# Stage six attention: the context scores as one product per head inside the row-tiled group, instead of one block-diagonal product

## The chip, the cores and the metric

The kernel runs on one core of a Trainium2 chip. It is written by hand, engine by engine: TensorE (PE), VectorE (DVE), ScalarE (ACT), GpSimd (POOL) and SyncE (SP) each have their own instruction list, and semaphores order them against one another. The metric is the device time of one execution in microseconds (us), the median of several executions.

## The reference, cut to what matters

The program is four layers, each of a gated cross attention and a gated feed-forward part, on x of shape 2 x 1024 x 256. They are computed as eight stages, 0 to 7. The change touches stage six, the cross attention of the last layer:

```
q = layer_norm(latents) @ Wq            # latents = layer-normed x, 2 x 1024 rows
kv = concat(layer_norm(ctx), layer_norm(latents)) @ Wkv
sim = einsum('bhid,bhjd->bhij', q * scale, k)     # 16 heads of 64
attn = softmax(where(mask, sim, max_neg))
out = einsum('bhij,bhjd->bhid', attn, v) @ Wout
```

So every one of the 1024 query rows of a batch element attends to 1101 columns: 1024 tokens (self) and 77 rows of context, and only the context columns can be masked. All is float32.

## The kernel before

Stage six walks over 128 units (`NU`). Unit u is one tile of 128 queries (`qt = u % 8`) of one pair of heads (`n = u // 8`; 8 pairs for each of the 2 batch elements). The two heads of a pair lie in the partitions 0 to 63 (head zero) and 64 to 127 (head one) of the query tile `s6_q`, the key tile `s6_k` and the context keys `s6_kx`.

The scores of a unit fill PSUM banks 0 to 4: head zero's 1024 token columns in banks 0 and 1, head one's in banks 3 and 4, and both heads' 77 context columns in bank 2, head zero's at its front and head one's at its end (`s6_both` is a view of both). So each head's 1101 columns are contiguous (`s6_sc`). PE's function `scores(u)` (L1146) waits until the exponentials of the unit before have been read out of these banks (`a6_p`), then multiplies:

- the context columns of both heads in one product over all 128 partitions. For this `s6_kx` is block-diagonal, 2 x 77 columns: head zero's keys stand in partitions 0 to 63 of the first 77 columns, head one's in partitions 64 to 127 of the other 77, and the rest is zero (a POOL memset at the start of the stage, L1852);
- four products of 512 token columns, each over the 64 partitions of one head.

DVE then takes the unit up. On the first signal of `a6_s` (the context product) it adds the mask to the context columns (L2465) and reduces them to a maximum for each head (L2466). On the second signal (the last token product) it reduces each head's 1024 token columns (L2470) and takes the lower of the two negated maxima (L2471); each of these two signals `a6_mx`. ACT exponentiates each head's 1101 columns (L1728) with that as bias and signals `a6_p`.

Five further steps run in the same loop on banks 5, 6 and 7, which rotate: a step takes the bank of the step three places before it in the list and waits until that one has been copied out (`free_bank`, L1139). In iteration u, PE does `scores(u)`; two turns (transposes) of unit u-1's exponentials, `p_turn` 0 and 1, copied out by ACT (L1717); in even u, two pieces of the projections of the next head pair (`piece`, numbers j = u % 8 and j+1); in odd u, `weigh`, the product of the attention with the values; then the turn of the context columns (`ctx_turn`, L1178 and L1179), `p_turn` 2 and 3, copied out by DVE (L2492); in even u the turn of the row sums (L1186). Of the two pieces, ACT copies out the first, j, and does so between the two exponentials of unit u; DVE copies out the second (L2411, L2410), after the maxima of unit u. The pieces by j = u % 8 are: 0: queries; 2: value tiles 0 and 1 together with the context keys, and keys; 4: value tiles 2 to 5, and keys; 6: value tiles 6 to 8, and keys. For the context keys ACT has two copies, one for each block of the diagonal (L1694, L1695). Units 120 to 127 have no pieces, and a few units (60 to 67, and from 124 on) have output projections and normalisations beside the rest.

On PE a float32 product shows in the trace as two passes, each a weight load (PEld) and a MATMUL record. `link` on DVE makes the engine wait for its own instruction; an instruction without it lets the next start before it ends.

Of the kernel before, what the change touches and what calls it, by code (L numbers as in the profile page):

```python
# [12 lines left out]
ALU = mybir.AluOpType  # L13
ACT = mybir.ActivationFunctionType
AX = mybir.AxisListType

P = 128
# [34 lines left out]
def build(nc, A, out, stages=ALL_STAGES):  # L52

    ctx = ExitStack()
    with ctx:
# [3 lines left out]
        def sem(name):  # L59
            return ctx.enter_context(nc.semaphore(name))  # L60
# [28 lines left out]
        def cut(region, at, *shape, rows=P, dt=F32):  # L89

            n = int(np.prod(shape))
            words = n if dt == F32 else n // 2
            v = region[0:rows, at:at + words]
            if dt != F32:
                v = v.bitcast(dt)
            if len(shape) == 2:
                v = v.rearrange("p (a b) -> p a b", a=shape[0])
            if len(shape) == 3:
                v = v.rearrange("p (a b c) -> p a b c", a=shape[0], b=shape[1])
            return v  # L100
# [107 lines left out]
        s6_wout = cut(WE, 0, 8, D)  # L208
        s6_wq, s6_wk, s6_wv = (cut(WE, 2048 * (i + 1), KD, 8 * P) for i in range(3))
        s6_gob = cut(WE, 8192, 2, D)  # L210
        s6_kx = [cut(WE, 8704 + 154 * i, 2, C) for i in range(2)]
        s6_mk = cut(WE, 9012, B, C)
        s6_p = [[cut(WO, 1536 + 1104 * (2 * i + h), 1104) for h in range(2)] for i in range(2)]
        s6_q = [cut(WO, 5952 + 1024 * i, S) for i in range(2)]
# [86 lines left out]
        c6_mm, c6_sb = sem("c6_mm"), sem("c6_sb")  # L301
        a6_s, a6_mx, a6_p, a6_rb, o6_sd = sem("a6_s"), sem("a6_mx"), sem("a6_p"), sem("a6_rb"), sem("o6_sd")
        r6_mm, r6_act, r6_dve = sem("r6_mm"), sem("r6_act"), sem("r6_dve")
        z6_in, g6_sb, x6_b = sem("z6_in"), sem("g6_sb"), sem("x6_b")
        q5_n, q5_s, q5_w, q5_b, q5_f = sem("q5_n"), sem("q5_s"), sem("q5_w"), sem("q5_b"), sem("q5_f")
        cn6_x, cn6_tr, cn6_f = sem("cn6_x"), sem("cn6_tr"), sem("cn6_f")
        m7, gc7_mm, gc7, f7_tr, f7_add = sem("m7"), sem("gc7_mm"), sem("gc7"), sem("f7_tr"), sem("f7_add")
# [298 lines left out]
        def _(pe):  # L606
            def mm(o, lhsT, rhs, start=True, stop=True, **kw):
                return pe.matmul(o, lhsT, rhs, start=start, stop=stop, **kw)  # L608
# [504 lines left out]
            def stage6():  # L1113
# [32 lines left out]
                def scores(u):  # L1146

                    n, qt = divmod(u, 8)
                    if qt == 0 and n == 0:
                        pe.wait_ge(c6_sb, 8)  # L1150
                    elif qt == 0:
                        copied(pe, ("w", n, 6))
                        copied(pe, ("w", n, 7))
                    if u:
                        pe.wait_ge(a6_p, 2 * u)
                    q0 = qt * P
                    mm(s6_both, s6_q[n % 2][:, q0:q0 + P], s6_kx[n % 2]).then_inc(a6_s, 1)
                    for i in range(2):
                        for h in range(2):
                            r = 64 * h  # L1160
                            last = mm(PS[:, 3 * h + i, :], s6_q[n % 2][r:r + 64, q0:q0 + P], s6_k[n % 2][r:r + 64, i * 512:(i + 1) * 512])
                    last.then_inc(a6_s, 1)

                def p_turn(u, i):

# [199 lines left out]
        def _(act):  # L1365
# [309 lines left out]
            def stage6():  # L1675
                tr = tr_no[6]
                act.wait_ge(w_in[6], 16 * 7)
                act.wait_ge(ln_var, ln_no[6] + 2)
                act.activation(lnsd[:, 8:NT], lnve[:, 8:NT], ACT.Sqrt).then_inc(ln_std, 1)
                act.wait_ge(ln_nb, half_no[6] + 1)  # L1680

                def piece(n, j, bank):

                    kind, lo, hi = PIECES[j]
                    if kind == "q":
                        return act.activation(s6_q[n % 2][:, lo:hi], PS[:, bank, :], ACT.Copy, scale=DH ** -0.5)
                    full = min(hi, 8) - lo
                    last = act.activation(s6_v[n % 2][:, lo:lo + full].rearrange("p a n -> p (a n)"), PS[:, bank, 0:full * P], ACT.Copy)
                    if hi == NKT:
                        last = act.activation(s6_v[n % 2][0:C, 8], PS[0:C, bank, full * P:full * P + P], ACT.Copy)  # L1690
                    if lo == 0:
                        if n < 2:
                            act.wait_ge(z6_in, 1)
                        act.activation(s6_kx[n % 2][0:64, 0], PS[0:64, bank, 2 * P:2 * P + C], ACT.Copy)  # L1694
                        last = act.activation(s6_kx[n % 2][64:P, 1], PS[64:P, bank, 2 * P:2 * P + C], ACT.Copy)  # L1695
                    return last

                def filled(key):

                    act.wait_ge(r6_mm, r6_no[key] + 1)  # L1700
                    return r6_bank(key)

                for j in range(0, 8, 2):
                    if j < 4:
                        for t in range(8 + 2 * j, 12 + 2 * j):
                            act.activation(XN[:, t, :], X[:, t, :], ACT.Identity, bias=ln_bias[:, t:t + 1], scale=lnrs[:, t:t + 1]).then_inc(ln_xa, 1)
                    act.wait_ge(c6_mm, j + 1)
                    piece(0, j, j).then_inc(c6_sb, 1)
                for u in range(NU + 5):
                    even = u % 2 == 0  # L1710
                    n, j = u // 8 + 1, u % 8
                    if 1 <= u <= NU:
                        v = u - 1
                        g, c0 = v // 2, (v % 2) * P
                        for i in range(2):
                            bank = filled(("p", v, i))
                            act.activation(s6_pt[g % 2][0][:, 4 * i:4 * i + 4, c0:c0 + P], PS[:, bank, :].rearrange("p (a n) -> p a n", a=4), ACT.Copy).then_inc(r6_act, 1)  # L1717
                    if u < NU:
                        g = u // 2
                        if u == 0:  # L1720
                            for i in range(2):
                                act.wait_ge(ln_tr, 8 * tr + 5 + i)
                                rows_copy6(2 + i, 5 + i)
                        if u >= 2:
                            act.wait_ge(r6_mm, r6_no["p", u - 2, 3] + 1)
                        for h in range(2):
                            act.wait_ge(a6_mx, 2 * u + h + 1)
                            act.activation(s6_p[u % 2][h][:, 0:KV], s6_sc[h], ACT.Exp, bias=s6_nm[:, u % 2, h:h + 1],  # L1728
                                           accum_out=s6_sm[:, g % 2, 2 * (u % 2) + h:2 * (u % 2) + h + 1]).then_inc(a6_p, 1)
                            if h == 0 and even and n < 16:  # L1730
                                piece(n, j, filled(("w", n, j))).then_inc(r6_act, 1)
                    if even and 2 <= u <= NU:
                        g = (u - 2) // 2
                        bank = filled(("r", g))
                        act.activation(s6_r[g % 2], PS[:, bank, 0:2 * P], ACT.Copy).then_inc(r6_act, 1)
                    if even and u >= 4 and (u // 2 - 2) % 32 >= 28:
                        g = u // 2 - 2
                        t = 8 * (g // 32) + 2 * (g % 4)
                        copied(act, ("o", g))
                        act.activation(lnsd[:, t:t + 2], lnve[:, t:t + 2], ACT.Sqrt).then_inc(o6_sd, 1)  # L1740
# [75 lines left out]
        def _(pool):  # L1816
# [31 lines left out]
            for s in stages:  # L1848
                if s in (1, 3):
                    expert_tiles(s)  # L1850
                if s == 6:
                    pool.memset(WE[:, 8704:9012], 0.0).then_inc(z6_in, 1)  # L1852
                    pool.wait_ge(g6_sb, 1)
                    pool.wait_ge(ln_xn, NT * (xn_no[ln_no[6]] + 1))
                    pool.wait_ge(ln_xa, 8 * half_no[6] + 8)
                    pool.tensor_tensor(X[:, :, :], X[:, :, :], s6_gob[:, 1].unsqueeze(1).broadcast_to([P, NT, D]), ALU.add).then_inc(x6_b, 1)
                meet(pool, s)
# [3 lines left out]
        def _(dve):  # L1861
            chain = [0]

            def link(ins):

                chain[0] += 1
                ins.then_inc(dve_chain, 1)
                dve.wait_ge(dve_chain, chain[0])
# [526 lines left out]
            def stage6():  # L2395
# [57 lines left out]
                for u in range(NU + 6):  # L2453
# [7 lines left out]
                            dve.wait_ge(r6_mm, r6_no["r", g - 2] + 1)  # L2461
                        dve.tensor_copy(s6_rb[g % 2], s6_rc[:, g % 2].unsqueeze(2).broadcast_to([P, 4, DH])).then_inc(a6_rb, 1)
                    if u < NU:
                        dve.wait_ge(a6_s, 2 * u + 1)
                        link(dve.tensor_tensor(s6_both, s6_both, s6_mk[:, u // 64].unsqueeze(1).broadcast_to([P, 2, C]), ALU.add))  # L2465
                        dve.tensor_reduce(s6_cm[:, u % 2], s6_both, AX.X, ALU.max, negate=True)  # L2466
                        dve.wait_ge(a6_s, 2 * u + 2)
                        for h in range(2):
                            m = s6_nm[:, u % 2, h:h + 1]
                            link(dve.tensor_reduce(m, s6_main[h], AX.X, ALU.max, negate=True))  # L2470
                            dve.tensor_tensor(m, m, s6_cm[:, u % 2, h:h + 1], ALU.min).then_inc(a6_mx, 1)  # L2471
                    if u == 0:
                        for i in range(2):
# [175 lines left out]
```

## Time and profile before

| | |
|---|---|
| median of 3 runs | 2306.05 us (2305.68 to 2307.14) |
| the profiled execution | 2320.85 us, of which its span is 2319.0 us |
| PE busy | 2138.4 us, 92% of the span |
| DVE busy | 1390.3 us, 60% |
| ACT busy | 1030.6 us, 44% |
| POOL busy | 129.3 us, 6% |

The span runs from the first instruction of the profiled execution to the last. A PE that shows busy is not necessarily at its peak, because the ends of matmuls are modelled; so the starts of its records say more than the busy share.

### The profile page before, as it was taken

What the parts mean: (1) busy time and instruction counts of PE and PEld (TensorE: products, weight loads), DVE (VectorE), ACT (ScalarE), POOL (GpSimd) and SP (SyncE); (2) the same over time, 40 slices, a digit from 0 to 9 for tenths busy, and PEclk for the clock granted to TensorE, in tenths of its full rate; (3) what the DMA queues carried; (4) which work ended last, traced back from release to release, by engine and by line L of the source; (5) the groups of instructions that cost most, each with busy time, mean ns of one, the idle gap of its engine ahead of it and who ended that gap; (6) DMA issues with size and microseconds to landing.
All of it is one profiled execution on the core that took longest, in us unless ns stands there. A gap on an engine that the chain in (4) does not pass through costs nothing. (4 is left out here: it accounts for less than half of the span.)

```text
span 2319.0 us, 34530 instructions
## 1 busy us (share of the span) xinstructions
PE 2138.4 (92%) x13157; PEld 1519.3 (66%) x13157; DVE 1390.3 (60%) x3046; ACT 1030.6 (44%) x2153; POOL 129.3 (6%) x122
## 2 busy tenths in 40 slices
PE   6996997968999799796999999999999999999988
PEld 4875996434999688555566666666666666666643
DVE  5763112672444678687576666666566666666555
ACT  5752442530112522487444445444444444544455
POOL 1002111005122000000100000000000000000000
PEclk8997999889999999898999999999999999999999
DMA  3605996024897600200000000000000000000001
GB/s 117 173 3 174 310 324 231 19 79 133 270 318 260 197 1 1 78 1 9 4 1 1 1 1 1 1 1 1 1 1 1 1 1 1 1 1 1 1 1 36
DMA packets 109262, 159.78 MB, mean 69 GB/s; under 512 B 12555, under 2 KB 85165, under 8 KB 109101
## 3 DMA queue, kind: packets, MB, share of 16 engines
q1 hardware_dynamic: 101805, 134.80, 17.7%
q0 software_dynamic: 7296, 22.78, 2.9%
q8 instruction: 107, 1.75, 0.3%
q14 instruction: 54, 0.44, 0.1%
HBM read 127.64 MB, written 29.91 MB: 68 GB/s over the span
## 5 line engine op out<-in xcount | busy, mean ns | idle before, releaser
L608 PE MATMUL ps<-arena,w_odd 128*128 128x128 f32 (+4 forms) x2352 | 437.3, 439 | 3.0 <-DVE arena L2149 1.2
L608 PE MATMUL ps<-arena 128*64 128x256 f32 (+4 forms) x3216 | 388.2, 371 | 8.3 <-DVE arena L2280 4.5
L2470 DVE TENSOR_REDUCE small<-ps 128x1 f32<-128x1024 f32 x256 | 312.5, 1221 | 86.5 <-PE ps L608 86.5
L1717 ACT ACTIVATE arena<-ps 128x512 f32<-128x512 f32 x256 | 139.1, 594 | 452.8 <-PE ps L1171 452.7
L608 PEld LDWEIGHTS ps<-arena 128*64 128x64 f32 (+4 forms) x3216 | 254.5, 154 | 120.1 <-issue 22.6
L608 PEld LDWEIGHTS ps<-arena,w_odd 128*128 128x128 f32 (+3 forms) x2352 | 245.9, 187 | 106.0 <-issue 100.8
L1728 ACT ACTIVATE w_odd<-ps,small 128x1101 f32<-128x1101 f32 x256 | 302.7, 1183 | 6.5 <-DVE small L2471 4.7
L1171 PEld LDWEIGHTS ps<-ident,w_odd 128*128 128x128 f32 x2048 | 223.1, 141 | 121.0 <-issue 110.4
L1171 PE MATMUL ps<-ident,w_odd 128*128 128x128 f32 x2048 | 281.6, 277 | 9.5 <-DVE arena L2411 3.1
L2492 DVE COPY arena<-ps 128x512 f32<-128x512 f32 x256 | 164.3, 683 | 4.1 <-PE ps L1171 1.7
L608 PE MATMUL ps<-xn_feat,w_even 128*128 128x512 f32 (+1 forms) x352 | 137.9, 523 | 5.1 <-DVE xn_feat L2393 2.3
L1518 ACT ACTIVATE arena<-ps,arena 128x128 f32<-128x128 f32 x184 | 67.4, 368 | 93.3 <-PE ps L608 82.7
L608 PE MATMUL ps<-arena,w_even 128*128 128x256 f32 (+2 forms) x608 | 107.7, 330 | 0.5 <-DVE x_res L1930 0.5
L608 PE MATMUL ps<-xn_feat,w_odd 128*128 128x512 f32 x224 | 103.7, 603 | 0.0
L608 PE MATMUL ps<-w_odd,arena 128*128 128x256 f32 (+1 forms) x436 | 101.5, 379 | 0.0
L608 PEld LDWEIGHTS ps<-arena,w_even 128*128 128x128 f32 x608 | 94.7, 192 | 8.6 <-DVE x_res L1930 0.6
L608 PE MATMUL ps<-w_even,xn_feat 128*128 128x128 f32 (+1 forms) x576 | 96.2, 313 | 0.0
L1538 ACT ACTIVATE arena<-ps 128x128 f32<-128x128 f32 (+1 forms) x117 | 32.3, 276 | 141.5 <-PE ps L608 139.7
L608 PEld LDWEIGHTS ps<-xn_feat,w_even 128*128 128x128 f32 x352 | 62.2, 192 | 45.1 <-issue 38.9
L2170 DVE TENSOR_SCALAR arena<-ps,arena 128x256 f32<-128x256 f32 x62 | 30.0, 484 | 96.8 <-PE ps L608 96.8
L608 PEld LDWEIGHTS ps<-w_odd,arena 128*128 128x128 f32 (+1 forms) x436 | 79.5, 190 | 9.0
L608 PEld LDWEIGHTS ps<-w_even,xn_feat 128*128 128x128 f32 x576 | 73.6, 192 | 17.0 <-issue 16.7
(386 smaller groups left out, 2928.8 us busy)
## 6 DMA issues: line engine op xcount, KB each, us to landing
w_odd<-in_s_w SPq DMA_DIRECT2D x32, 1024.0 KB
w_odd<-in_s_wgu SPq DMA_DIRECT2D x30, 704.0 KB
w_even<-in_s_w SPq DMA_DIRECT2D x15, 1024.0 KB
arena<-expert_rows_in SPq DMA_DIRECT2D x62, 130.0 KB
w_odd<-in_s_wd SPq DMA_DIRECT2D x30, 256.0 KB
out_feat<-in_s_wgu SPq DMA_DIRECT2D x10, 704.0 KB, 4.2
expert_rows_in<-zero_row POOLq DMA_DIRECT2D x1, 5070.0 KB, 32.5
vo_rows<-w_odd SPq DMA_DIRECT2D x8, 616.0 KB
```

Source lines behind the costliest of these rows:

```text
L608: return pe.matmul(o, lhsT, rhs, start=start, stop=stop, **kw)
L1171: last = pe.transpose(PS[:, bank, j * P:(j + 1) * P], src[:, c0:c0 + P], ident[:, :])
L1518: act.activation(s1_h[q][:, m], PS[:, (M * i + m) % 4, 0:TS], ACT.Gelu, bias=s1_bt[w][:, m:m + 1]).then_inc(per["mu_act", 1], 1)
L1538: act.activation(s3_s[0:rows, u % 2, 0:TS], PS[0:rows, u % 4, 0:TS], ACT.Silu).then_inc(per["mu_act", 3], 1)
L1717: act.activation(s6_pt[g % 2][0][:, 4 * i:4 * i + 4, c0:c0 + P], PS[:, bank, :].rearrange("p (a n) -> p a n", a=4), ACT.Copy).then_inc(r6_ ...
L1728: act.activation(s6_p[u % 2][h][:, 0:KV], s6_sc[h], ACT.Exp, bias=s6_nm[:, u % 2, h:h + 1], accum_out=s6_sm[:, g % 2, 2 * (u % 2) + h:2 * ...
L2170: dve.tensor_scalar(mx_y[st][v % 2][:, j], PS[:, 4 + n % 2, 0:D], es_xg[:, v, 1:2], None, ALU.mult).then_inc(per["md_sb", st], 1)
L2470: link(dve.tensor_reduce(m, s6_main[h], AX.X, ALU.max, negate=True))
L2492: dve.tensor_copy(s6_pt[g % 2][1][:, 4 * (i - 2):4 * (i - 2) + 4, c0:c0 + P], PS[:, bank, :].rearrange("p (a n) -> p a n", a=4)).then_inc( ...
```

## The change

The context keys lose their zero blocks: `s6_kx` becomes one tile of 77 columns, head zero's in partitions 0 to 63 and head one's in 64 to 127, copied out of PSUM by one ACT instruction instead of two. The memset and its semaphore go. The block-diagonal product becomes two products over 64 partitions each: head one's ahead of the four token products, head zero's behind them, with a wait on PE between that holds head zero's until head one's is complete, since both write bank 2. The four token products keep their order. DVE takes up the mask only on the second signal of `a6_s`, the one of head zero's context product; the mask addition is no longer linked, the reduction of the context columns moves behind that of head zero's token columns, and it is linked.

```diff
-        s6_kx = [cut(WE, 8704 + 154 * i, 2, C) for i in range(2)]
+        s6_kx = [cut(WE, 8704 + C * i, C) for i in range(2)]
...
-                    mm(s6_both, s6_q[n % 2][:, q0:q0 + P], s6_kx[n % 2]).then_inc(a6_s, 1)
-                    for i in range(2):
-                        for h in range(2):
-                            r = 64 * h
-                            last = mm(PS[:, 3 * h + i, :], s6_q[n % 2][r:r + 64, q0:q0 + P], s6_k[n % 2][r:r + 64, i * 512:(i + 1) * 512])
-                    last.then_inc(a6_s, 1)
+
+                    def main(h, i):
+
+                        r = 64 * h
+                        return mm(PS[:, 3 * h + i, :], s6_q[n % 2][r:r + 64, q0:q0 + P], s6_k[n % 2][r:r + 64, i * 512:(i + 1) * 512])
+
+                    def context(h):
+
+                        r = 64 * h
+                        return mm(PS[:, 2, (512 - C) * h:(512 - C) * h + C], s6_q[n % 2][r:r + 64, q0:q0 + P], s6_kx[n % 2][r:r + 64])
+
+                    context(1).then_inc(a6_s, 1)
+                    main(0, 0)
+                    main(1, 0)
+                    main(0, 1)
+                    main(1, 1)
+                    pe.wait_ge(a6_s, 2 * u + 1)
+                    context(0).then_inc(a6_s, 1)
...
-                        if n < 2:
-                            act.wait_ge(z6_in, 1)
-                        act.activation(s6_kx[n % 2][0:64, 0], PS[0:64, bank, 2 * P:2 * P + C], ACT.Copy)
-                        last = act.activation(s6_kx[n % 2][64:P, 1], PS[64:P, bank, 2 * P:2 * P + C], ACT.Copy)
+                        last = act.activation(s6_kx[n % 2], PS[:, bank, 2 * P:2 * P + C], ACT.Copy)
...
-                    pool.memset(WE[:, 8704:9012], 0.0).then_inc(z6_in, 1)
...
-                        dve.wait_ge(a6_s, 2 * u + 1)
-                        link(dve.tensor_tensor(s6_both, s6_both, s6_mk[:, u // 64].unsqueeze(1).broadcast_to([P, 2, C]), ALU.add))
-                        dve.tensor_reduce(s6_cm[:, u % 2], s6_both, AX.X, ALU.max, negate=True)
                         dve.wait_ge(a6_s, 2 * u + 2)
+                        dve.tensor_tensor(s6_both, s6_both, s6_mk[:, u // 64].unsqueeze(1).broadcast_to([P, 2, C]), ALU.add)
                         for h in range(2):
                             m = s6_nm[:, u % 2, h:h + 1]
                             link(dve.tensor_reduce(m, s6_main[h], AX.X, ALU.max, negate=True))
+                            if h == 0:
+                                link(dve.tensor_reduce(s6_cm[:, u % 2], s6_both, AX.X, ALU.max, negate=True))
                             dve.tensor_tensor(m, m, s6_cm[:, u % 2, h:h + 1], ALU.min).then_inc(a6_mx, 1)
```

## Rows read from the trace of the kernel before

**Rows 1.** Windows view, all units of stage six: length, busy (instructions) per engine, clock.
```profile
1108.50:2190.80 1082.30, 1062.28 (x7083) 702.54 (x7083) 722.50 (x1471) 518.42 (x957) 2.62 (x1) 1.00 0.00 1
```

**Rows 2.** Waits view of stage six: who waited for whom, total us, times, longest.
```profile
DVE small L2470 <- PE ps L608: 86.5, 117, 2.2
```

**Rows 3.** Matmul records of stage six by operands and shape: ns min/median/max.
```profile
L608 PE MATMUL ps<-arena,w_odd x1024: 589/589/1057, 1108.5 to 2181.8; 64*128 64x512 f32 x171
...
L608 PE MATMUL ps<-w_even,w_odd x256: 294/294/398, 1108.0 to 2180.2; 128*128 128x154 f32 x128
...
L608 PE MATMUL ps<-arena,w_even x64: 232/275/275, 1100.3 to 2068.7; 128*128 128x77 f32 x64
```

**Rows 4.** Timeline, scores of unit 36 (start us, us): PE and DVE.
```profile
1402.36 1.04 PE L1171 MATMUL ps<-ident,w_odd 128*128 128x128 f32 x8
...
1403.23 0.43 PE L608 MATMUL ps<-w_even,w_odd 128*128 128x154 f32 x2
...
1403.59 1.99 PE L608 MATMUL ps<-arena,w_odd 64*128 64x512 f32 x8
...
1404.61 0.32 DVE L2465 TENSOR_TENSOR ps<-ps,w_even 128x154 f32<-128x154 f32 x1
1404.97 0.32 DVE L2466 TENSOR_REDUCE small<-ps 128x2 f32<-128x154 f32 x1
...
1405.51 1.09 PE L1171 MATMUL ps<-ident,w_odd 128*128 128x128 f32 x8
```

**Rows 5.** Timeline, unit 34: the context keys' product, 77 columns a pass.
```profile
1390.86 0.57 PE L608 MATMUL ps<-arena,w_even 128*128 128x77 f32 x4
```

**Rows 6.** Timeline, unit 36 (j = 4) after its scores: DVE, ACT, then PE.
```profile
1405.62 1.22 DVE L2470 TENSOR_REDUCE small<-ps 128x1 f32<-128x1024 f32 x1 [0.34 <-PE ps L608]
...
1406.88 0.16 DVE L2471 TENSOR_TENSOR small<-small 128x1 f32<-128x1 f32 x1
1406.96 1.22 DVE L2470 TENSOR_REDUCE small<-ps 128x1 f32<-128x1024 f32 x1
1407.17 1.19 ACT L1728 ACTIVATE w_odd<-ps,small 128x1101 f32<-128x1101 f32 x1
...
1408.23 0.21 ACT L1728 ACTIVATION_READ_ACCUMULATOR w_odd<-ps,small 128x1 f32 x1
1408.42 0.60 ACT L1688 ACTIVATE arena<-ps 128x512 f32<-128x512 f32 x1
...
1409.20 0.47 PEld L1171 LDWEIGHTS ps<-ident,w_odd 128*128 128x128 f32 x4
...
1409.31 1.18 PE L1171 MATMUL ps<-ident,w_odd 128*128 128x128 f32 x8
...
1409.83 0.42 PEld L1171 LDWEIGHTS ps<-ident,w_odd 128*128 128x128 f32 x4 [0.16 <-issue]
```

**Rows 7.** Timeline, unit 38 (j = 6): ACT's copy, the turn behind it, next scores.
```profile
1424.39 0.28 ACT L1690 ACTIVATE arena<-ps 77x128 f32<-77x128 f32 x1
...
1424.78 0.86 PEld L1171 LDWEIGHTS ps<-ident,w_odd 128*128 128x128 f32 x8 [0.20 <-issue]
...
1425.94 0.47 PE L608 MATMUL ps<-w_even,w_odd 128*128 128x154 f32 x2
```

**Rows 8.** Timeline, unit 34 (j = 2): ACT's last copy, the turn behind it.
```profile
1392.35 0.23 ACT L1695 ACTIVATE w_even<-ps 64x77 f32<-64x77 f32 x1
...
1393.13 0.47 PEld L1171 LDWEIGHTS ps<-ident,w_odd 128*128 128x128 f32 x4
```

**Rows 9.** Timeline, odd unit 37: its last ACT instruction, the next scores.
```profile
1416.80 0.19 ACT L1728 ACTIVATION_READ_ACCUMULATOR w_odd<-ps,small 128x1 f32 x1
...
1419.03 0.43 PE L608 MATMUL ps<-w_even,w_odd 128*128 128x154 f32 x2
```

**Rows 10.** Timeline, unit 120 (no pieces): its last exponential, the next scores.
```profile
2118.26 0.19 ACT L1728 ACTIVATION_READ_ACCUMULATOR w_odd<-ps,small 128x1 f32 x1
...
2118.51 0.30 PEld L608 LDWEIGHTS ps<-w_even,w_odd 128*128 128x128 f32 x2 [0.71 <-ACT w_odd L1728]
```

More of the change, by code:

```diff
@@ L303, in build @@
         r6_mm, r6_act, r6_dve = sem("r6_mm"), sem("r6_act"), sem("r6_dve")
-        z6_in, g6_sb, x6_b = sem("z6_in"), sem("g6_sb"), sem("x6_b")
+        g6_sb, x6_b = sem("g6_sb"), sem("x6_b")
         q5_n, q5_s, q5_w, q5_b, q5_f = sem("q5_n"), sem("q5_s"), sem("q5_w"), sem("q5_b"), sem("q5_f")
```

## The prediction, made before the changed kernel was run

> **What bounds the kernel now.** I read the windows of stage six first, then its waits, then the matmul records by shape, then the timeline of single units. The stage lasts 1082.3 us and holds PE for 1062.3 of them, at a granted clock of 1.00 throughout [rows 1]: PE's order of work sets the time, and there is no clock to win or lose. But busy ends are modelled, so the gaps between PE's starts decide, and these show where another engine sets the pace. The waits view shows the cover that the change gives up: in 117 of the 128 units DVE waits for PE at the first long reduction [rows 2], so in these the mask addition and the context maximum lie beside PE's token products and cost nothing. The units repeat with a period of eight, so the timeline of one unit of each kind stands for all (units 34, 36, 38: j = 2, 4, 6; unit 37 for the odd ones).
>
> **PE's part of the change.** In rows 4 the block-diagonal product starts at 1403.23; its two passes take 0.13 each (0.43 less one record of 0.29 [rows 3]), to 1403.50. The token products' record starts at 1403.59, 0.09 after. Its eight passes of 0.43 last 1.99, not 3.4: the two heads run side by side, four in a row (1.72); the rest is one record's tail and 0.11 in which the first weights are loaded. So the token columns stream from 1403.70 to 1405.42, and the next transposes begin 0.09 after. From the end of the old transposes to head one's token columns: 0.47.
>
> After: the array still changes from 128 rows to 64 and back, so 0.09 and 0.11 stay. Head one's two context passes follow, and head one's token columns behind them; head zero's token columns start at once and its context passes fill the same length behind. The trace of before has no 77-column pass over 64 rows. The nearest row is the product of the context keys, 77 columns over 128 rows: four records in 0.57, less one of 0.23, is 0.11 a pass [rows 3, 5]. That is not half of 0.13, although half as many columns stream: the pass lasts as long as the loading of the next weights (128 columns have 0.11 too, [rows 4]: 1.04 less 0.27, by seven). The ends are 0.07 (half of 0.13, columns alone) and 0.11; I take 0.11, since the 64-row products also spend 0.11 on their first weights. Then 0.09 + 0.11 + 2 x 0.11 = 0.42: PE gains 0.05 a unit, 6.4 us in 128. By 0.07 it gains 0.13 to 0.14, 17.5 us.
>
> The Trainium skill (TensorE: Matmul & The Clock Gate, LDWEIGHTS) speaks against the change here: a load is priced by its columns, 128 / 1.2 = 107 ns, and one of 32 rows takes as long as one of 128. By that rule two 77-column passes are an estimated 0.21, and halving the rows brings nothing back; the trace agrees with the 0.11 of its 128-row rows, and no row of before shows it for 64 rows.
>
> The wait on PE ahead of head zero's context product costs nothing in the sum: head one's product is complete some 0.5 after the start, and the array needs head zero's not before 1.7. Behind it on PE are the turns, which come after it anyway. The bound above is rival D.
>
> **DVE's part.** All of its work on a unit now starts after the last product. The mask (0.32, no longer linked) lets its successor start 0.08 before its end, as L2471 does [rows 6]: 0.24. The context maximum, linked, stands ahead of head zero's bias: 0.32 + 0.03 (0.36 from start to start for the linked mask [rows 4]): 0.35. Both maxima come 0.59 later than now, counted from the end of the scores. The first exponential perhaps a little less: it starts 0.13 after its maximum [rows 6], part of which is ACT's own copying, and the last signal may come 0.04 before head one's end. Ends 0.50 and 0.59; I take 0.54 for what hangs on the first exponential, 0.59 for the second where nothing stands between.
>
> **Who waits for that.** ACT, in order: exponential of head zero, copy of piece j, exponential of head one. PE's `p_turn` 2 needs the bank of piece j, so:
> - j = 4 [rows 6]: the copy ends at 1409.02, PE comes at 1409.20. Now it ends at 1409.56, and PE's load follows a copy by 0.11 ([rows 7]: 1424.67 to 1424.78), at 1409.67: 0.47 late. The wait that PE has today between the two turns (1.18 against 1.04 for eight passes [rows 4, 6]: 0.14) is then over. Net 0.33.
> - j = 6 [rows 7]: PE already waits for this copy. The 0.54 is paid in full, less the 0.04 by which the next scores' record is long today (0.47 against 0.43 [rows 4]): 0.50.
> - j = 2 [rows 8]: ACT's last copy ends at 1392.58, PE comes at 1393.13, a slack of 0.44 beside the hand-over. The change also merges two copies (0.24 saved). 0.54 less 0.24 fits: nothing. j = 0 has longer pieces and more slack: nothing.
> - odd units [rows 9]: the last exponential ends at 1416.99, the next scores start at 1419.03. Slack of 2: nothing.
> - units without pieces (120, 122, 124, and unit 1): the next scores wait for the second exponential itself [rows 10], as the load at 2118.51 stands 0.06 behind its end. Full 0.59, less some 0.2, as the array has then drained and the 0.09 and more are covered: 0.40 over the general account, 1.6 in all.
>
> There are 15 units of j = 4 and 15 of j = 6. In one of each I expect nothing, since among the 11 units in which DVE does not wait for PE [rows 2] it is late already and only does the same work in another order. So 14 x 0.33 = 4.6 and 14 x 0.50 = 7.0; with 1.6: 13.2 us lost, 6.4 gained, +6.8. The merged copy and the memset lie on engines that wait anyway (ACT is busy for 518 of 1082 [rows 1]): nothing. On the profiled execution, 2320.85 becomes 2327.7; the same step on the median, which lies 14.8 below it, 2306.05 to 2312.8.
>
> **Rivals.**
> A (forecast): PE gains 0.05 a unit and the waits of j = 4 and 6 take 13.2: 2312.8, own range 2310 to 2315.5.
> B (the other side, not slower): context passes over 64 rows follow the columns, 0.07 each. Place: the start of each unit's scores. Gain 17.5 against 13.2: -4.3, 2301.8. It decides from a pass below 0.08, where gain and loss meet. For it: the token products at 0.43 show no load at all. Against: the 0.11 of rows 5. The Trainium skill (TensorEngine Tiling (Array Packing), Theoretical Speedup) gives up to twice the rate for a contraction of 64 rows or fewer, which is B's direction.
> C (cover larger than I count): DVE's lateness is 0.50, j = 4 takes up more in the small waits that follow it, and unit 124 and unit 1 hide theirs behind their other work: 4 + 6.3 + 0.8 less 6.4, +4.7 or less; with passes of 0.10 (another 0.02 a unit) +2: 2308 to 2310.7, at 2309.5.
> D: the wait on PE, or the order of passes, keeps head zero's context product from lying beside head one's tokens: 2 x 0.11 a unit behind them, 28 us more, 2341. Against it: the passes of two heads start as pairs although the program lists one head's two passes before the other's ([rows 4]: 1.99 for eight), so each half of the array has its own order.
>
> **Chances.** A 0.57, B 0.13, C 0.22, D 0.08. A difference of 0.2% (4.6 us) is about what a measurement of this kernel can tell from none. Below 2301.4: half of B and a little of C's tail, 0.10. Above 2310.7: most of A, D and a fifth of C, 0.62. Between: 0.28. The range 2301 to 2316 leaves out D and the edges of A and B.
>
> **What would show it.** PE's start of the transposes behind the scores comes 2.23 instead of 2.28 after the old ones' end. In PE's weight loads over 64 rows, the two of head one's context stand 0.11 apart; 0.07 would be B. The first maximum starts its wait for PE at the mask addition (L2465), not at L2470. Exponentials start 2.7 after the last token record instead of 2.2. In units of j = 4 and 6 PE's turn of head one waits for ACT (L1688, L1690) by 0.4 to 0.6; in j = 0, 2 and odd units PE's order shows no new gap. The forecast is wrong if the periods of j = 4 and 6 don't grow, or if the odd units shrink by more than 0.1 each.

## The result, and the profile after

The changed kernel takes 2316.72 us (median of 6 runs, 2315.89 to 2318.47), beside 2306.6 us for the kernel before (6 runs, 2304.48 to 2308.84): ratio 1.0043, 95% interval 1.0032 to 1.0054. That is slower by 10.1 us. The forecast was slower by 6.8, and the time lies 0.7 us above the range.

The page after, PE's line, and the windows view of its stage six up to the last token record (columns as in rows 1):

```profile
PE 2131.1 (92%) x13413; PEld 1606.6 (69%) x13413; DVE 1389.5 (60%) x3046; ACT 1038.4 (45%) x2137; POOL 128.4 (6%) x121
...
1095.00:2177.70 1082.70, 1049.91 (x7268) 785.34 (x7269) 714.80 (x1457) 520.43 (x932) 3.13 (x1) 0.99 0.00 1
```

[Rows 1] runs 9 us further, so the same stretch of before is:

```profile
1108.50:2181.90 1073.40, 1053.38 (x7013) 696.39 (x7012) 715.78 (x1457) 512.23 (x947) 2.62 (x1) 1.00 0.00 1
```

PE has 3.5 us less to do, and its idle time has grown from 20.0 to 32.8 us. The clock reads 0.99 instead of 1.00: a small difference in a mean over 1082 us, and the part that I missed.

The stretches of stage six, each from the start of the first token record of one unit to that of a later one (the third ends with the start of the stage's last token record, the fourth with the span), worked out from both traces. What lies ahead of the stage took 13 us longer in the profiled execution of before, and would hide the difference in a comparison of whole spans:

| us | units 0 to 2 | 3 to 119 | 120 to 127 | behind, to the end |
|---|---|---|---|---|
| before | 28.34 | 975.55 | 69.48 | 137.11 |
| after | 29.07 | 979.88 | 73.65 | 138.05 |
| difference | +0.7 | +4.3 | +4.2 | +0.9 |

The sum, 10.2, lies beside the 10.1 of the medians, though each trace is a single execution. The 117 regular units hold less than half of it; the last eight hold as much.

The token records of stage six, after (columns as in rows 3), and DVE's wait for them (as in rows 2):

```profile
L608 PE MATMUL ps<-arena,w_odd x1024: 588/590/1217, 1095.0 to 2177.6; 64*128 64x512 f32 x171
```

```profile
DVE ps L2473 <- PE ps L608: 150.1, 117, 3.6
```

DVE's wait has moved from the long reduction to the mask addition, as forecast, again 117 times, and has grown from 86.5 to 150.1 us: 0.54 a unit. The longest token record is 1217 ns, against 1057 before and a median of 590.

The scores of unit 38 after, timeline (start, length, engine):

```profile
1407.06 1.04 PE L1183 MATMUL ps<-ident,w_odd 128*128 128x128 f32 x8
1408.03 0.18 PEld L608 LDWEIGHTS ps<-w_even,w_odd 64*128 64x128 f32 x1 [0.17 <-issue]
1408.03 0.33 PE L608 MATMUL ps<-w_even,w_odd 64*128 64x77 f32 x1
...
1408.14 0.19 PEld L608 LDWEIGHTS ps<-w_even,w_odd 64*128 64x128 f32 x1
1408.20 0.27 PE L608 MATMUL ps<-w_even,w_odd 64*128 64x77 f32 x1
1408.31 1.92 PE L608 MATMUL ps<-arena,w_odd 64*128 64x512 f32 x7
1409.86 0.34 PE L608 MATMUL ps<-w_even,w_odd 64*128 64x77 f32 x2
...
1410.16 1.09 PE L1183 MATMUL ps<-ident,w_odd 128*128 128x128 f32 x8
```

The next transposes begin 2.06 behind the end of the old ones (1410.16, 1408.10), against 2.11 in [rows 4] (1405.51, 1403.40): 0.05 less, as between the forecast's 2.23 and 2.28, which count from the start of the scores. The two context loads of head one stand 0.11 apart. Head zero's context passes (1409.86) run beside head one's last tokens.

What follows in the unit before it, unit 36 (j = 4), timeline of DVE, ACT and PE:

```profile
1394.26 1.09 PE L1183 MATMUL ps<-ident,w_odd 128*128 128x128 f32 x8
...
1394.38 0.33 DVE L2473 TENSOR_TENSOR ps<-ps,w_even 128x154 f32<-128x154 f32 x1 [0.89 <-PE ps L608]
1394.62 1.22 DVE L2476 TENSOR_REDUCE small<-ps 128x1 f32<-128x1024 f32 x1
...
1395.86 0.32 DVE L2478 TENSOR_REDUCE small<-ps 128x2 f32<-128x154 f32 x1
1396.22 0.16 DVE L2479 TENSOR_TENSOR small<-small 128x1 f32<-128x1 f32 x1
1396.47 1.18 ACT L1737 ACTIVATE w_odd<-ps,small 128x1101 f32<-128x1101 f32 x1 [0.44 <-DVE small L2479]
...
1397.64 0.59 ACT L1700 ACTIVATE arena<-ps 128x512 f32<-128x512 f32 x1
...
1398.34 0.85 PEld L1183 LDWEIGHTS ps<-ident,w_odd 128*128 128x128 f32 x8 [0.35 <-issue]
1398.37 1.06 PE L1183 MATMUL ps<-ident,w_odd 128*128 128x128 f32 x8 [0.15 <-ACT arena L1700]
```

0.24 for the mask and 0.36 for the context maximum, as forecast. And unit 38 (j = 6), PE:

```profile
1414.19 0.85 PEld L1183 LDWEIGHTS ps<-ident,w_odd 128*128 128x128 f32 x8 [0.75 <-ACT w_odd L1737]
1414.22 1.06 PE L1183 MATMUL ps<-ident,w_odd 128*128 128x128 f32 x8 [0.55 <-ACT arena L1702]
```

The gap in front of the turn, named 0.20 in [rows 7], is 0.75 now. The median periods of the units 3 to 119, from first token record to first token record, by j (before, after): j = 0 8.363, 8.314; j = 2 7.987, 7.941; j = 4 7.310, 7.462; j = 6 6.951, 7.404; odd 8.49, 8.443. So each unit is 0.045 to 0.05 shorter, apart from j = 4, 0.15 longer, and j = 6, 0.45 longer.

Now the tail of the stage. First the windows of after (length, busy of PE, PEld, DVE, ACT, POOL, granted clock), then those of before around its own last units:

```profile
1116.00:1126.00 10.00, 9.78 (x53) 7.20 (x51) 5.43 (x10) 4.30 (x9) 0.00 (x0) 0.85 0.01 2
...
2100.00:2120.00 20.00, 18.03 (x141) 13.05 (x137) 13.26 (x27) 9.96 (x17) 0.00 (x0) 1.00 0.01 1
2120.00:2140.00 20.00, 17.91 (x120) 13.27 (x117) 12.58 (x26) 8.41 (x15) 0.00 (x0) 0.91 0.00 1
2140.00:2160.00 20.00, 18.44 (x108) 14.08 (x107) 9.45 (x23) 9.28 (x15) 0.00 (x0) 0.91 0.00 1
2160.00:2180.00 20.00, 17.71 (x94) 13.94 (x94) 11.47 (x28) 6.47 (x11) 0.00 (x0) 0.91 0.00 1
```

```profile
2130.00:2150.00 20.00, 17.52 (x119) 11.43 (x118) 14.23 (x28) 12.04 (x21) 0.00 (x0) 1.00 0.00 1
2150.00:2170.00 20.00, 18.58 (x118) 12.93 (x116) 12.07 (x29) 7.18 (x12) 0.00 (x0) 1.00 0.00 1
2170.00:2190.00 20.00, 18.99 (x108) 13.96 (x109) 9.34 (x24) 8.96 (x16) 0.00 (x0) 0.91 0.00 1
```

Before, one window of the tail is below 1.00; after, three in a row are. The timeline says what 0.91 is. The end of the loop pass in front of the scores of unit 123 after, then the same gap before:

```profile
2122.95 1.12 PE L1183 MATMUL ps<-ident,w_odd 128*128 128x128 f32 x8
2125.44 0.41 PE L1198 MATMUL ps<-ident,arena 128*128 128x128 f32 x2 [1.37 <-DVE arena L2497]
2126.32 0.49 PE L608 MATMUL ps<-w_even,w_odd 64*128 64x77 f32 x1 [0.47 <-ACT w_odd L1737]
...
2126.82 3.21 PE L608 MATMUL ps<-arena,w_odd 64*128 64x512 f32 x7
```

```profile
2132.72 0.41 PE L1186 MATMUL ps<-ident,arena 128*128 128x128 f32 x2 [0.79 <-DVE arena L2489]
2133.60 0.53 PE L608 MATMUL ps<-w_even,w_odd 128*128 128x154 f32 x2 [0.47 <-ACT w_odd L1728]
2134.06 1.99 PE L608 MATMUL ps<-arena,w_odd 64*128 64x512 f32 x8
```

The gap ahead of the transposes of the row sums (`sums_turn`) is 0.79 before and 1.37 after: DVE's 0.58. Behind the longer gap the record of seven token passes takes 3.21 instead of 1.92 (see unit 38): TensorE is at the lower of its levels, 1.2 of 2.4 GHz. A window of 20 us that reads 0.91 holds an estimated 3.6 us at half clock (0.09 of 20, doubled), which loses half of that. So the wait costs its own length and then some 1.5 us more. Not every such wait does: in the last units of this trace PE waits three times for 1.37 or 1.38 us, and the clock falls behind the second and the third only.

### The profile page after: what moved, and what is told of

Its sections match the earlier page's. It is cut to its first block and busy times, and to the rows that moved or that the text cites. A ratio compares the mean times of both kernels' runs of the same rounds, so it can differ in the third digit from the quotient of the medians.

```text
span 2315.7 us, 35026 instructions
## 1 busy us (share of the span) xinstructions
PE 2131.1 (92%) x13413; PEld 1606.6 (69%) x13413; DVE 1389.5 (60%) x3046; ACT 1038.4 (45%) x2137; POOL 128.4 (6%) x121
## 5 line engine op out<-in xcount | busy, mean ns | idle before, releaser
L608 PE MATMUL ps<-arena,w_odd 128*128 128x128 f32 (+4 forms) x2352 | 464.9, 437 | 3.0 <-DVE arena L2157 1.2
L608 PEld LDWEIGHTS ps<-arena,w_odd 128*128 128x128 f32 (+3 forms) x2352 | 319.4, 188 | 39.3 <-issue 19.7
L2476 DVE TENSOR_REDUCE small<-ps 128x1 f32<-128x1024 f32 x256 | 311.5, 1217 | 0.0
L2473 DVE TENSOR_TENSOR ps<-ps,w_even 128x154 f32<-128x154 f32 x128 | 41.8, 326 | 150.9 <-PE ps L608 150.1
L608 PEld LDWEIGHTS ps<-w_even,w_odd 64*128 64x128 f32 x512 | 86.3, 187 | 62.1 <-issue 48.2
L608 PE MATMUL ps<-w_even,w_odd 64*128 64x77 f32 x512 | 100.5, 277 | 3.8 <-ACT w_odd L1737 3.2
```

## The experiments

The theory after this reading: (a) DVE's lateness costs 0.2 in units of j = 4 and 0.5 in those of j = 6; (b) in the units without pieces, at both ends of the stage, the longer gaps let the clock fall, 1.5 to 1.7 us each. The rivals: (b') the tail is only more waiting, as forecast; (c) the product's new form on PE itself costs something. All times are medians, beside the kernel before measured together with each.

**e1: PE's new form, with the maxima early.** Head zero's context product between the two halves of the token products, DVE as before.

```diff
-                    main(0, 1)
-                    main(1, 1)
-                    pe.wait_ge(a6_s, 2 * u + 1)
+                    pe.wait_ge(a6_s, 3 * u + 1)
                     context(0).then_inc(a6_s, 1)
+                    main(0, 1)
+                    main(1, 1).then_inc(a6_s, 1)
```
(and DVE's part as before the change, waiting for `3 * u + 2` and `3 * u + 3`)

> The changed kernel with head zero's context product moved from behind the four token products to between them (head one's context, tokens 0/0 and 1/0, wait, head zero's context, tokens 0/1 and 1/1), three signals of a6_s a unit, and DVE as in the kernel before: linked mask and context maximum ahead of the long reductions. It takes the late start of DVE away and keeps all of PE's part. Theory (PE gains 0.05 a unit, the late maxima cost the rest): each unit is 0.05 shorter than before, j = 4 and 6 too, 6.4 us less in all, 2300 +-1.5. Rival 1 (the wait inside the row-tiled group costs: the half of the array that waits stands still): units 0.1 to 0.4 longer, 13 to 50 us more. Rival 2 (the context signal now comes about 1.3 after the first weights instead of 0.2, so DVE ends its context work after the token products): maxima 0.05 to 0.15 late, nothing in most units because of slack, j = 6 +0.1 and the last units: 2301 to 2303.

Measured: 2300.07 us beside 2306.35, ratio 0.997 (0.9958 to 0.9982). Each unit is 0.04 shorter than before, those of j = 6 0.09, and the 117 units take 970.10. PE and DVE in a unit of e1, timeline:

```profile
1400.45 1.06 PE L608 MATMUL ps<-arena,w_odd 64*128 64x512 f32 x3
1401.14 0.34 PE L608 MATMUL ps<-w_even,w_odd 64*128 64x77 f32 x2
1401.32 1.06 PE L608 MATMUL ps<-arena,w_odd 64*128 64x512 f32 x4
...
1401.57 0.33 DVE L2473 TENSOR_TENSOR ps<-ps,w_even 128x154 f32<-128x154 f32 x1
```

The mask addition lies beside the second half of the token products again. Rival (c) falls: the row tiles bring 0.04 to 0.05 a unit, and the order that gives up DVE's cover takes it away. **This version beats both kernels**, the one before by 6.3 us and the changed one by some 16.

**e2: the kernel before with DVE's part of the change alone**, the block-diagonal product kept.

```diff
-                        dve.wait_ge(a6_s, 2 * u + 1)
-                        link(dve.tensor_tensor(s6_both, ...))
-                        dve.tensor_reduce(s6_cm[:, u % 2], ...)
                         dve.wait_ge(a6_s, 2 * u + 2)
+                        dve.tensor_tensor(s6_both, ...)
...
+                            if h == 0:
+                                link(dve.tensor_reduce(s6_cm[:, u % 2], ...))
```

> The kernel before with DVE's part of the change alone: block-diagonal product on PE as before, mask and context maximum only after the last token product, in the changed order. Theory: the whole loss without PE's gain: j = 4 +0.20, j = 6 +0.50, units 120 to 127 +4 to +5, all other units unchanged; +15 to +17, 2322 to 2324. Rival (the row-tiled products themselves cost something that hides behind the waits, so that DVE's share is smaller): +10 or less, and PE's share in the sum positive.

Measured: 2327.45 beside 2306.35, ratio 1.009 (1.0076 to 1.0104): +21.1, more than either theory gave. In the trace j = 4 grows by 0.24, j = 6 by 0.54, the others by 0.00; units 3 to 119 take 986.69, +11.1; units 120 and 122 grow by 0.57 each, the length of the wait, and units 121 and 123, behind it, by 1.65 and 1.70. The traced execution is the fastest of the five (2324.52) and lies 16.6 over the one of before from the stage's first token record on; the other 4.5 of the 21.1 stand in no trace. With e1 and the two kernels the regular units make a square: late maxima cost 11.1 with the old product (986.69 less 975.55) and 9.8 with the new (979.88 less 970.10); the row tiles give 5.5 and 6.8.

**e3 and e9: late only in the last eight units, or only ahead of them.** Both branch on the unit's number around e2's edit.

```diff
+                        if u >= 120:      # e3; e9: if u < 120
...
+                        else:
```

> The kernel before with DVE's late order in units 120 to 127 only (those without pieces). Theory (the longer waits there let the clock of TensorE fall once or twice more, about 1.7 us each time, besides the waits): granted clock below 1.00 in two or three stretches of 10 us instead of one, +3.5 to +6, 2310 to 2313. Rival (waits alone: 0.59 less cover in units 120, 122 and 124, clock as before): +1.2 to +1.8, 2308.

> The kernel before with DVE's late order in units 0 to 119 only: the complement of the run in which only the last eight units were late. Theory (waits of 0.24 in j = 4 and 0.54 in j = 6 as the profile of the kernel with all units late shows, 15 of the one with 0.33 in unit 60, 14 of the other, and about 1 in units 0 to 2; the clock of the last eight as in the kernel before): +11 to +13, 2317.5 to 2320, and granted clock below 1.00 in at most one stretch among the last eight units. Rival (the excess of the late kernel over its waits comes from somewhere else than its last eight units): +15 or more, 2321 to 2324.

Measured: e3 2310.61 beside 2306.35, ratio 1.0019 (1.001 to 1.0028), +4.3. Lateness in eight units, in which mere waiting was put at 1.2 to 1.8, costs as much as theory (b) says. e9: 2321.61 beside 2306.14, ratio 1.0066 (1.0052 to 1.0079), +15.5, above the 11 to 13 that the theory gave and in the rival's region. The trace places 11.2 in units 3 to 119 (986.77), and 2.6 in units 0 to 2 (29.47 against 26.83 in e5, where the clock holds in unit 2); the window of 1116 to 1126 reads 0.89 there. So the clock falls at the start of the stage too, where the expectation had about 1. Against the trace of before, which has that fall in unit 2 as well (28.34), only 1.1 of it is left: of five profiles with early maxima at the start that of before alone has it, against all six with late maxima and no filler there. Together e3 and e9 give 19.8 of e2's 21.1.

**e4, e5, e6, e8: five thrown-away transposes in the gap** of units 119, 121, 123 and 125, in the changed kernel (e4), the one before (e5), e2 (e6) and e1 (e8). They add work to PE where it waits, and nothing else. Each transpose shows as one record of the trace, not as two passes as the expectation of e4 has it.

```diff
                     src = s6_p[u % 2][i // 2]
+                    if i == 3 and u in (119, 121, 123, 125):
+                        for _ in range(5):
+                            pe.transpose(PS[:, bank, 0:P], src[:, 512 + C:512 + C + P], ident[:, :])
```

> The changed kernel with five further transposes of the same columns into the same bank (10 passes of 0.11, work that is thrown away) ahead of the last turn of units 119, 121, 123 and 125, where PE otherwise waits some 1.4 us for DVE. Theory (clock): the granted clock stays 1.00 from unit 120 to at least 125 and the kernel takes 3 to 4.5 us less than the changed one, 2312 to 2314, although it has more to do. Rival (the clock has nothing to do with it, the last units wait for DVE and ACT): no gain, or 0.2 to 0.5 us more than the changed kernel.

> The kernel before with the filler of the last experiment (five more transposes of the same columns ahead of the last turn of units 119, 121, 123 and 125). Theory (falls of the granted clock among the last eight units are part of every one of these times, one in most executions of the kernel before): clock 1.00 there, 0.5 to 2 us less than before, 2304.5 to 2306. Rival (no falls there in most executions, or the filler delays the turn): equal to before or up to 0.5 us more.

> Block-diagonal product on PE as before, DVE's late order, and the filler. Theory (the waits cost 13 and the clock the rest of the 21 that the same kernel without filler cost): 2318 to 2320, that is 12.5 to 14 over the filled kernel before and 6 to 7 over the filled changed kernel (2311.9), PE's gain of 0.05 a unit. Rival (the 21 are waits that the profiled executions don't show): 2325 to 2328, no gain by the filler.

> Head zero's context product between the token products, DVE as before, and the filler in the last units: both remedies together. Theory: 6.4 us below the filled kernel before and 12 to 13 below the filled changed kernel, 2298 to 2300. Rival (the first of the two remedies lives on the same time as the filler): 2300 or more, no better than without filler.

| | us | before | ratio (95%) | against the same without filler |
|---|---|---|---|---|
| e4 | 2311.9 | 2306.35 | 1.0026 (1.0015 to 1.0036) | 4.8 less than after |
| e5 | 2307.79 | 2306.99 | 0.9997 (0.9988 to 1.0006) | no less than before |
| e6 | 2320.22 | 2306.99 | 1.0055 (1.0041 to 1.0069) | 7.2 less than e2 |
| e8 | 2300.65 | 2306.99 | 0.9968 (0.9956 to 0.998) | no less than e1 |

e4 and e6 lie 0.1 and 0.2 outside what the theory gave (2312 to 2314, 2318 to 2320). The gains that it gave for early maxima, in e5 and e8, did not come; e8 landed in its rival's range. PE's gap and the windows of e4's tail:

```profile
2122.11 0.74 PE L1183 MATMUL ps<-ident,w_odd 128*128 128x128 f32 x5
2122.68 0.60 PE L1186 MATMUL ps<-ident,w_odd 128*128 128x128 f32 x4
...
2124.11 0.41 PE L1201 MATMUL ps<-ident,arena 128*128 128x128 f32 x2 [0.83 <-DVE arena L2500]
...
2125.27 1.92 PE L608 MATMUL ps<-arena,w_odd 64*128 64x512 f32 x7
```

```profile
2120.00:2140.00 20.00, 17.53 (x132) 13.10 (x129) 14.63 (x30) 10.83 (x18) 0.00 (x0) 1.00 0.00 1
2140.00:2160.00 20.00, 19.79 (x127) 15.55 (x128) 11.12 (x27) 7.97 (x14) 0.00 (x0) 1.00 0.00 1
2160.00:2180.00 20.00, 18.20 (x119) 14.07 (x118) 11.09 (x27) 9.95 (x16) 0.00 (x0) 1.00 0.00 1
```

The five transposes take 0.57 from start to start (2122.11 to 2122.68), and the gap reads 0.83, close to before's 0.79; the token passes behind it take 1.92, and the clock is 1.00. Units 120 to 127 take 69.07 instead of 73.65: 4.6 of the 4.8. Rival (b') falls, since adding matmuls to a waiting engine would leave the time as it was. Over all the profiles the lengths sort the falls, though not one by one: with late maxima and no filler (after, e2, e3, e7) each tail has three gaps of 1.36 to 1.38, and the clock falls behind two of them; behind the 21 gaps of 0.78 to 0.83 (before, e1, e9, e4, e6, e10, e11) it never does. The same window in e2 and in e6:

```profile
2120.00:2140.00 20.00, 18.04 (x102) 9.59 (x99) 10.48 (x22) 7.52 (x13) 0.00 (x0) 0.85 0.00 1
```

```profile
2120.00:2140.00 20.00, 18.59 (x140) 11.73 (x137) 13.10 (x26) 11.14 (x19) 0.00 (x0) 1.00 0.00 1
```

Two falls in e2 (0.85, 102 matmuls), none in e6 (140). A warning for readers: PE's busy share is 18.04 in the one and 17.53 in e4's, and tells nothing, because a matmul at half clock is busy for longer. Where the maxima are early (e5, e8) the filler gives nothing, though all three profiles with early maxima and no filler in the tail (before, e1, e9) show a fall in unit 126, and those of e5 and e8 none (1.68 less there in e5).

The granted clock of every execution is on record too, as a mean over the whole of it. It is 0.9634 and 0.9630 for before (19 and 16 executions), 0.9607 after, 0.9600 in e2; with filler 0.9640 in e4 and 0.9636 in e6. So late maxima cost clock, and the filler gives it back, in all the executions and not in the traced ones alone. In e5 it reads 0.9632, as before: what the filler saves in the tail of that trace is no gain over the whole. In e8 it is 0.9633 against 0.9625 in e1, without a gain in time. Where it goes, no run shows.

**e7: head products of 128 columns instead of 77.** Zero columns beside the 77 (tiles of 179 words, cleared once).

```diff
-                        return mm(PS[:, 2, (512 - C) * h:...], s6_q[...], s6_kx[n % 2][r:r + 64])
+                        at = (P - C) * (1 - h)
+                        return mm(PS[:, 2, (512 - P) * h:...], s6_q[...], s6_kx[n % 2][r:r + 64, at:at + P])
```

> The changed kernel with 128 columns instead of 77 in each head's context product: 51 zero columns beside the 77, in the middle of bank 2 where nothing reads them (the memset is back for them). Theory (a pass of the context product lasts as long as the load of the next weights, 0.11, whatever its columns up to 128): 66% more columns for nothing, PE's weight loads over 64 rows still 0.11 apart, time equal to the changed kernel within 1 us. Rival (a pass lasts as long as its columns, 0.064 and 0.107): 0.09 a unit, +11 us; half of that if only one of the two heads' passes is exposed.

Measured: 2318.39 beside 2306.99, ratio 1.0048 (1.0034 to 1.0062), 1.3 more over its own before than the changed kernel; by the times as they stand 1.7 more than the changed kernel, a little outside the expected 1. The periods differ by 0.003 a unit. The scores of one of its units:

```profile
1400.93 0.37 PE L608 MATMUL ps<-w_even,w_odd 64*128 64x128 f32 x1
1400.93 0.69 PE L608 MATMUL ps<-arena,w_odd 64*128 64x512 f32 x1
1401.14 0.27 PE L608 MATMUL ps<-w_even,w_odd 64*128 64x128 f32 x1
1401.25 1.88 PE L608 MATMUL ps<-arena,w_odd 64*128 64x512 f32 x7
1402.76 0.38 PE L608 MATMUL ps<-w_even,w_odd 64*128 64x128 f32 x2
```

51 columns more in each pass cost nothing in the periods: head one's passes, ahead of its token passes, are paced by the loads, 0.11 apart. Rival B rested on the columns. Head zero's two passes, at the end, do follow them (two records in 0.34 after and in 0.38 here, less one of 0.27: 0.07 and 0.11), but they lie beside head one's tokens, where that brings nothing.

**e10 and e11: a filler at unit 0 as well**, nine transposes, in the changed kernel (e10) and in e2 (e11).

```diff
-                    if i == 3 and u in (119, 121, 123, 125):
-                        for _ in range(5):
+                    if i == 3 and u in (0, 119, 121, 123, 125):
+                        for _ in range(5 if u else 9):
```

> The changed kernel with the filler of the last units and nine more thrown-away transposes ahead of the last turn of unit 0, where PE waits 2.3 us before the scores of unit 2. Theory (in all six profiles with late maxima unit 2 lasts 9.6 instead of 8.0, and there the granted clock falls, against one of five with early maxima: the wait before it is the reason): unit 2 lasts 8.0, 1 to 2 us less than the kernel filled in its last units only (2311.9), 2310 to 2311. Rival (the longer unit 2 is due to the first projections, not to the wait): unit 2 stays at 9.6, 2312.

> Block-diagonal product on PE, DVE's late order, and the filler at both ends of the stage. Theory: 1 to 2 us less than with the filler in the last units only (2320.2), 2318 to 2319.5, and 8 +-1 over the changed kernel filled at both ends (PE's 6.4 and the noise of both). Rival: unit 2 at 9.6, 2320.

Measured: e10 2314.66 beside 2308.09, ratio 1.003 (1.002 to 1.004); e11 2320.48 beside 2308.09, ratio 1.0056 (1.0042 to 1.007). Both missed their theories, and e10 its rival too. Unit 2 lasts 7.94 in e10 and 7.99 in e11, against 9.56 to 9.63 in all six kernels with late maxima and no filler there. So the fall at unit 2 is gone in both profiles, but the time doesn't follow: over its own before, e10 stands at +6.6 where e4 stood at +5.5, and e11 at +12.4 where e6 stood at +13.2. The windows of e10's last units:

```profile
2140.00:2160.00 20.00, 19.43 (x123) 15.05 (x124) 11.12 (x29) 8.44 (x14) 0.00 (x0) 1.00 0.00 1
2160.00:2180.00 20.00, 18.20 (x105) 13.85 (x106) 9.45 (x22) 8.74 (x14) 0.00 (x0) 0.91 0.00 1
```

In this profile the fall that was removed at unit 2 stands in the tail instead (70.76 in the last eight units against e4's 69.07), and what follows the stage takes 138.98 instead of 136.91. The mean clock of its nine executions is 0.9632, no better than the 0.9640 of e4's eight, so the clock won at unit 2 is lost again elsewhere. Why, stays open.

## Why the prediction was right or wrong

**PE's gain, 0.05 a unit: right.** 0.045 to 0.05 in every unit without a wait; 0.11 a pass by the loads, as e7 bears out. Rival B is refuted.

**DVE's lateness: right.** 0.24 + 0.36 for 0.59; the first exponential starts 2.21 behind the transposes' first start instead of 1.66, 0.55 where I took 0.54.

**j = 6, +0.50 before PE's gain: right,** 0.45 net. **j = 4, +0.33: too large;** 0.15 + 0.05 = 0.20. In [rows 6] the copy of piece 4 starts at 1408.42, 1.25 behind the exponential's start; after, it starts 1.17 behind (1396.47 to 1397.64). Before, it had waited for PE's piece, as its start 0.03 behind the end of that piece (1408.39) suggests, so 0.08 of the lateness had a cover on ACT that I took for none. The other 0.05 lies in the hand-over behind the copy, which I can't split further. That is 0.13 in 14 units, 1.8 us, the other way from the miss. Hence units 3 to 119: forecast 11.6 less 5.8, +5.8; measured +4.3.

**j = 0, 2, odd units: right**, no new gap. **Rival D: refuted**; head zero's context product runs beside head one's tokens (1409.86 above).

**The step that failed is in the first paragraph: "at a granted clock of 1.00 throughout [rows 1]: ... there is no clock to win or lose".** From it came "0.40 each, 1.6 in all" for the units without pieces. The rows give 1.00 as a mean over 1082 us, which hides a few stretches of 3 to 4 us at half the clock: before has three of its own (units 0, 2 and 126), which lower that mean by an estimated 0.005, and after five (units 0, 2, 123, 124 and 126). The one in unit 0 stands in every profile; windows of 10 us read 0.83 there, before and after. As waits, those 0.40 were near: with the clock held (e4 against e5), units 120 and 122 grow by 0.34, which is 0.39 before PE's gain, and unit 124 by 0.54. The eight last units and the first three were forecast at about +1; they cost +4.9 in the profiles against before, and 8.1 against e5, which has no fall in either place but that of unit 0. In the last eight, against before, 1.3 of the 4.2 is waiting less PE's gain (69.07 in e4 against 67.79 in e5), and 2.9 is clock: three falls for one. e3 (+4.3 for eight units) and e4 (4.8 back by filling) show it in the medians. With the tail filled, the changed kernel stands 5.5 above before, close to the 6.8 of a forecast that knew only waits.

So the 3.3 us between forecast and result are: 1.5 too much in units 3 to 119 (j = 4 by 1.8); 3.4 too little in the last units (4.2 against 0.8) and 0.5 in the first; and 0.9 behind the stage, for which I had no term. There, too, the clock is lower: 0.78 and 0.96 in the windows 2200 to 2220 and 2220 to 2240, against 0.83 and 1.00 in e4, where that stretch takes 136.91. In e6, filled as well, it takes 138.08, so its cause is open. That these terms add up to the difference of the medians is partly luck: each comes from one execution, and before's trace has falls in units 2 and 126 that e5's has not.

**The Trainium skill (TensorE: Matmul & The Clock Gate, LDWEIGHTS)** prices a load by its columns, an estimated 0.21 for two passes; the trace agrees, for 64 rows too, with loads 0.11 apart (1408.03, 1408.14). The Trainium skill (TensorEngine Tiling (Array Packing), Theoretical Speedup) gives up to twice the rate for 64 rows: the traces agree for the 512-column passes of two heads (eight of 0.43 in 1.99, [rows 4]), but not for those of 77, which gained 0.05 a unit.

## What to carry to other kernels

Before work is taken out from beside a long product, look for whose cover it was: here 0.05 a unit on the busiest engine was bought with 0.55 on the one that sends the next step off, and e1 shows that an order existed which kept both. A mean clock of 1.00 over a long stage is no proof that the clock can't be lost; look at windows of 10 to 20 us where an engine already waits, since a wait that grew by 0.58 us there cost some 1.5 us more behind it, two times in three. Where such a gap can't be closed, a few useless transposes in it are worth trying, but judge them by the median of several executions, since a clean profile did not always bring time.

## What the runs showed of the hardware

- A gap that grew from 0.79 to 1.37 us, with another of 0.47 behind it, was followed by a stretch at half the granted clock in eight of twelve cases (after, e2, e3, e7), at a cost of some 1.5 us (3.21 for 1.92 in unit 123 after). With five transposes in it, which left 0.83, there was none in twelve (e4, e6, e10, e11). So transposes, too, kept the clock up here.
- Where each of two 64-row passes waits for its weights (loads 0.11 us apart), 77 columns cost as much as 128: the periods differ by 0.003 us. Where nothing is loaded behind them, their starts stand 0.07 and 0.11 apart.
- The two row halves keep orders of their own: head zero's first token pass starts with head one's first context pass (1400.93 in e7) and ahead of head one's second (1401.14), though the program lists it behind both.
